# Eight-batch macaron block on one core: two layer tiles moved into the next batch's attention, tile-major normed activations, column-wise output-weight loads, weight splits moved into the schedule

## The reference, cut to what matters

```python
x = x + 0.5 * ffn(layernorm(x), w_router, w_block)
x = x + attn(layernorm(x), Wq, Wk_down, Wv_down, q_to_latent, v_up, Wout)
x = x + 0.5 * ffn(layernorm(x), w_router, w_block)

def ffn(x, w_router, w_block):          # k = 768 of 1024 tokens
    top_idx = top_k(x @ w_router, k)
    out = x; out[top_idx] = gelu(x[top_idx] @ w_block)

def attn(h, ...):                       # 16 heads of 32, latent of 64
    Q = h @ Wq.T; latent_k = h @ Wk_down.T; latent_v = h @ Wv_down.T
    logits = (Q @ q_to_latent) @ latent_k.T / 8, causal
    heads = softmax(logits) @ latent_v @ v_up
    return heads @ Wout.T
```

## Time and profile before

| | |
|---|---|
| runs (median) | 2641.53 us (2641.37 to 2642.27) |
| profiled execution, its own time | 2636.39 us |
| its span in the trace | 2634.7 us |
| mean granted TensorE clock | 0.958 of full speed |
| PE busy | 2351.9 us, 89% |
| DVE busy | 1724.5 us, 65% |
| ACT busy | 1164.1 us, 44% |
| POOL busy | 398.5 us, 15% |

### The profile page before, as it was taken

How to read it: one execution, slowest core, us unless ns; L and a number is a source line. 1 busy time by engine, 2 the same in 40 slices (tenths; PEclk the granted TensorE clock), 3 DMA queues, 4 the chain that set the end, 5 groups by cost and what they waited for, 6 DMA issues and landing times.

```text
span 2634.7 us, 53568 instructions
## 1 busy us (share of the span) xinstructions
PE 2351.9 (89%) x21888; PEld 1462.2 (55%) x21888; DVE 1724.5 (65%) x4806; ACT 1164.1 (44%) x2057; POOL 398.5 (15%) x510
## 2 busy tenths in 40 slices
PE   3769999899998998899988999989999899998976
PEld 2534466545674456745566456654466545674445
DVE  3668656785568855678556866668646785568725
ACT  3325543355434644246433454335543355434442
POOL 0101011112111121021111111111021112111121
PEclk9879999899998999989998999989999899998998
DMA  4100011100111002010020101110011100101000
GB/s 152 64 1 2 2 65 65 65 2 2 65 65 65 2 18 80 33 66 2 21 77 36 63 2 49 49 69 30 2 65 65 65 2 2 65 33 65 2 1 32
DMA packets 42482, 106.19 MB, mean 40 GB/s; under 512 B 2432, under 2 KB 3968, under 8 KB 38400
## 3 DMA queue, kind: packets, MB, share of 16 engines
q1 hardware_dynamic: 42240, 102.77, 11.0%
HBM read 64.49 MB, written 37.75 MB: 39 GB/s over the span
## 4 chain that ended last, share of the span: by engine, by line
PE 74%; DVE 12%; ACT 6%; issue 6%; POOL 1%; DMA 1%; SPq 0%; DVEq 0%; POOLq 0%; ACTq 0%
PE psum L704 30%; PE psum L717 18%; PE psum L823 8%; PE psum L830 7%; PE psum L720 4%; ACT pr L685 4%; DVE psum L958 3%; PE psum L731 3%; PE psum L746 3%; DVE junk L908 2%; DVE junk L906 1%; DVE nt_l L894 1%; DVE part L956 1%; DVE junk L910 1%; ACT nt_h L607 1%
## 5 line engine op out<-in xcount | busy, mean ns | idle before, releaser
L685 ACT ACTIVATE pr<-psum 128x512 f32<-128x512 f32 x1152 | 617.7, 596 | 627.7 <-PE psum L720 627.6
L717 PE MATMUL psum<-qk,qk 32*128 32x512 f32 (+3 forms) x4608 | 526.3, 376 | 100.8 <-ACT pr L685 38.4
L958 DVE CUSTOM_DVE_ANT_0 psum<-psum,mask_b 128x512 f32<-128x512 f32 (+3 forms) x1024 | 473.1, 523 | 142.7 <-PE psum L731 141.2
L717 PEld LDWEIGHTS psum<-qk,qk 32*128 32x128 f32 x4608 | 328.5, 190 | 414.2 <-ACT pr L685 122.8
L731 PE MATMUL psum<-qk,qk 32*128 32x512 f32 (+3 forms) x4608 | 527.6, 380 | 32.2 <-DVE qk L940 12.0
L956 DVE TENSOR_REDUCE part<-psum 128x1 f32<-128x512 f32 x512 | 325.3, 682 | 65.2 <-PE psum L731 63.6
L731 PEld LDWEIGHTS psum<-qk,qk 32*128 32x128 f32 x4608 | 319.9, 192 | 59.2 <-issue 18.2
L823 PE MATMUL psum<-pr,v_sb 128*32 128x512 f32 (+3 forms) x3072 | 316.8, 508 | 1.6 <-ACT acc_sb L607 1.6
L599 POOL TENSOR_SCALAR_AFFINE_SELECT pr<-pr 128x512 f32<-128x512 f32 x256 | 158.1, 636 | 1051.4 <-ACT pr L685 1051.4
L830 PE MATMUL psum<-pr,ones 128*32 128x512 f32 (+3 forms) x3072 | 306.2, 493 | 0.0
L720 PE MATMUL psum<-mrow,minus 1*128 1x512 f32 (+3 forms) x1536 | 223.2, 354 | 0.8 <-issue 0.8
(11 more groups left out here) (115 smaller groups left out, 3382.6 us busy)
## 6 DMA issues: line engine op xcount, KB each, us to landing
x<-x_dram SPq DMA_DIRECT2D x16, 1024.0 KB, 7.0
spill_x<-x SPq DMA_DIRECT2D x16, 1024.0 KB, 5.2
x<-spill_x SPq DMA_DIRECT2D x16, 1024.0 KB, 7.1
out_dram<-x SPq DMA_DIRECT2D x16, 1024.0 KB, 4.7
w_h<-scratch_o SPq DMA_DIRECT2D x7, 1024.0 KB, 4.8
w_l<-scratch_o SPq DMA_DIRECT2D x7, 1024.0 KB, 6.8
w_h<-scratch_q SPq DMA_DIRECT2D x6, 1024.0 KB, 4.9
w_l<-scratch_q SPq DMA_DIRECT2D x6, 1024.0 KB, 8.2
```

The costliest lines, as they stand in the source:

```text
L685: nc.scalar.activation(pr_of(b, g, u)[:, 2 * p + place, :], bank(e, place), ACT.Exp, scale=SCALE).then_inc(exp_ready, 1)
L717: eng.matmul(o, (k_h, k_h, k_l)[t][own, P * j:P * (j + 1)], (q_h, q_l, q_h)[t][own, queries], start=(t == 0 and at == 0), stop=False, skip ...
L958: m = nc.vector.tensor_tensor_reduce(scores, scores, mask_b[:, BANK - w:BANK], 1.0, FAR, ALU.add, ALU.max, top_of)
```

## The change

- **Layer tiles 6 and 7 of the second layer** (`F`, `G` with f = 1) of all batches but the last go from the end of `back(b)` to the first two chunks of group 0 of batch b+1: tile 6 behind the first `S` pair, tile 7 and both gelus behind the second. They use banks 6 and 7. The exp slots are dealt in the order 0, 2, 1, 3, so that the first two units overwrite tiles 0 to 3 only; the exp of unit 0 waits for `F` 3 and that of unit 2 for `F` 7.
- **The tiles of normed activations** become [P, NT, NK, P]: a token tile is one run of 512 elements. What reads 512 tokens at once (`SC`, `LAT`, `Q`) reads four runs of 128.
- **Order in `back`**: the router's `SC`, the maxima units 7 and 8, `SCOL` and the ranks `RT` move. `SCOL` has one `F` fewer ahead of it; `RT` 2 to 7 stand behind `F` 5.
- **Order in `project`**: `CB`, `ST` of tile 7 and the second half's norm factors go behind `T` 3; the `K`, `V`, `Q`, `MX` steps are dealt anew; the output weights are loaded in four column groups of 128, each as soon as `Q` of that group is done.
- **Weight splits** become steps `WS` of the list: router weights ahead of the first `NO`, layer weights behind `T` 4, latent, key/value and output weights ahead of the ranks, query weights behind the norm factors of the second norm.

```diff
     def front(b):
-        out += [("NO", 0, b, 0), ("NO", 0, b, 1)]
+        out += [("WS", 0), ("NO", 0, b, 0), ("NO", 0, b, 1)]
         for i in range(NT):
             out += [("T", 0, b, i)] + ([("NO", 0, b, i + 2)] if i + 2 < NT else [])
             out += [("SC", 0, b, i // TC)] if i % TC == TC - 1 else []
+            out += [("WS", 1)] if i == TC else []
...
     def project(b, left):
-        out += [] if b else [("RT", 0, b, i) for i in range(NT)] + [("RF", 0, b)] + [("GX", 0, b, i) for i in range(NT)]
+        out += [] if b else [("WS", 2), ("WS", 3), ("WS", 4)] + [("RT", 0, b, i) for i in range(NT)] + [("RF", 0, b)]
+        out += [] if b else [("GX", 0, b, i) for i in range(NT)]
         out += layer(0, b, 2) + layer(0, b, 3) + summed(b, 0) + summed(b, 1)
-        out += layer(0, b, 4) + summed(b, 2) + summed(b, 3) + scales(1, b, 0)
+        out += layer(0, b, 4) + summed(b, 2) + summed(b, 3) + scales(1, b, 0) + ([] if b else [("WS", 5)])
...
-        after = [summed(b, 6), summed(b, 7) + scales(1, b, 1), [], []]
+        after = [summed(b, 6), [], [], summed(b, 7) + scales(1, b, 1)]
...
-        for n in range(NQ):
-            out += (keys[0] + splits[0] + keys[1] + splits[1] if n == 0 else keys[n + 1] + splits[n + 1] if n < 3 else [])
-            out += [("Q", b, n, 1)] + (maxima(b, 0, n) if n < 3 else [])
-        out += [("W2", b - 1, "o")] if b else []
-        out += maxima(b, 0, 3)
-        for n in range(TC, NT):
-            out += keys[n] + splits[n] + (maxima(b, 0, 4) if n == TC + 1 else [])
+        loads = [[("W2", b - 1, "o", g)] if b else [] for g in range(NQ)]
+        out += keys[0] + splits[0] + keys[1] + splits[1] + [("Q", b, 0, 1)] + loads[0]
+        out += keys[2] + splits[2] + [("Q", b, 1, 1)] + loads[1] + maxima(b, 0, 0) + splits[3]
+        out += [("Q", b, 2, 1)] + loads[2] + maxima(b, 0, 1) + keys[3] + [("Q", b, 3, 1)] + loads[3] + maxima(b, 0, 2)
+        out += keys[4] + splits[4] + keys[5] + splits[5] + maxima(b, 0, 3)
+        out += keys[6] + splits[6] + keys[7] + splits[7] + maxima(b, 0, 4)
...
     def back(b):
-        out += layer(1, b, 0) + turn(3)[:1] + scales(2, b, 1) + [("SC", 1, b, 0)] + more(maxima, 7)
-        out += [("NO", 2, b, 4), ("NO", 2, b, 5)] + layer(1, b, 1) + turn(4) + turn(5) + more(maxima, 8)
-        out += layer(1, b, 2) + turn(6) + turn(7) + layer(1, b, 3) + [("SC", 1, b, 1)] + more(gathered, 0)
-        out += layer(1, b, 4) + [("SCOL", 1, b)] + more(turned, 0) + [("RT", 1, b, 0), ("RT", 1, b, 1)]
-        for i in range(5, NT):
-            out += layer(1, b, i) + [("RT", 1, b, 2 * (i - TC)), ("RT", 1, b, 2 * (i - TC) + 1)]
+        out += layer(1, b, 0) + turn(3)[:1] + scales(2, b, 1) + [("NO", 2, b, 4), ("NO", 2, b, 5)]
+        out += layer(1, b, 1) + turn(4) + turn(5) + [("SC", 1, b, 0)] + more(maxima, 7) + turn(6) + turn(7)
+        out += layer(1, b, 2) + [("SC", 1, b, 1)] + more(maxima, 8) + layer(1, b, 3) + [("SCOL", 1, b)] + more(gathered, 0)
+        out += layer(1, b, 4) + [("RT", 1, b, 0), ("RT", 1, b, 1)] + more(turned, 0)
+        out += layer(1, b, 5) + [("RT", 1, b, i) for i in range(2, NT)]
+        if b + 1 == B:
+            out += layer(1, b, 6) + layer(1, b, 7)
...
         if b > 0:
+            groups[0][0] += [("F", 1, b - 1, 6)]
+            groups[0][1] += [("F", 1, b - 1, 7), ("G", 1, b - 1, 6), ("G", 1, b - 1, 7)]
...
+        elif k == "F" and e[3] >= 6 and e[2] + 1 < B:
+            own = banks[e] = [e[3]]
...
-        nt_h = [over(f"nt{n}_h", region[n], [P, NK, T], F32R) for n in range(3)]
+        nt_h = [over(f"nt{n}_h", region[n], [P, NT, NK, P], F32R) for n in range(3)]
...
-            return prs[(b + 2) % 3][:, step_nth[b, g, u] % SLOTS, :, :]
+            return prs[(b + 2) % 3][:, (0, 2, 1, 3)[step_nth[b, g, u] % SLOTS], :, :]
...
                 elif k == "W2":
                     if which == "o":
-                        sp.wait_ge(q_done, last_q * (b + 2))
+                        sp.wait_ge(q_done, nth["Q", b + 1, g, 1])
+                        cols = slice(P * g, P * (g + 1))
-                    eng.dma_start(w2_h[:].bitcast(F32), src[0]).then_inc(w2_in, 16)
-                    eng.dma_start(w2_l[:].bitcast(F32), src[1]).then_inc(w2_in, 16)
+                    eng.dma_start(w2_h[:, :, cols].bitcast(F32), src[0][:, :, cols]).then_inc(w2_in, 16)
+                    eng.dma_start(w2_l[:, :, cols].bitcast(F32), src[1][:, :, cols]).then_inc(w2_in, 16)
...
-                    if (g, u) == (0, 0) and b:
-                        act.wait_ge(f_done, nth["F", 1, b - 1, NT - 1])
+                    if g == 0 and u in (0, 2) and b:
+                        act.wait_ge(f_done, nth["F", 1, b - 1, TC - 1 if u == 0 else NT - 1])
...
-                           lambda t, n: t[:, n, c * BANK:(c + 1) * BANK]).then_inc(sc_done, 1)
+                           lambda t, n: t[:, TC * c:TC * (c + 1), n, :]).then_inc(sc_done, 1)
```

More of the change, by code:

```diff
@@ L367, in macaron @@
         parts = [[over(f"qk{n}_{m}", region[n] + 4096 * m, [P, T], F32R) for m in range(8)] for n in range(3)]
-        nt_h = [over(f"nt{n}_h", region[n], [P, NK, T], F32R) for n in range(3)]
-        nt_l = [over(f"nt{n}_l", region[n] + 16384, [P, NK, T], F32R) for n in range(3)]
-        nt_act = [over(f"nt{n}_act", region[n], [P, NK, T]) for n in range(3)]
+        nt_h = [over(f"nt{n}_h", region[n], [P, NT, NK, P], F32R) for n in range(3)]
+        nt_l = [over(f"nt{n}_l", region[n] + 16384, [P, NT, NK, P], F32R) for n in range(3)]
+        nt_act = [over(f"nt{n}_act", region[n], [P, NT, NK, P]) for n in range(3)]
         prs = [over(f"pr{n}", region[n], [P, SLOTS, HQ, BANK]) for n in range(3)]
@@ L475, in macaron @@
         w2_loads = [e for e in sched if e[0] == "W2"]
-        w2_nth = {e: n + 1 for n, e in enumerate(w2_loads)}
-        last_q, last_o = NQ * NC, NT
+        w2_nth = {e: 32 * (n + 1) for n, e in enumerate(w2_loads)}
+        last_o = NT
         block = ctx.enter_context(nc.Block())
@@ L590, in _ @@
                     high, low = nt_of(2, b)
-                    cols = slice(c * BANK, (c + 1) * BANK)
+                    own = slice(TC * c, TC * (c + 1))
                     pool.wait_ge(hsh_ready, nth[e])
-                    nc.gpsimd.tensor_tensor(low[:, g, cols], ht[:, g, cols], high[:, g, cols].bitcast(F32), ALU.subtract
+                    nc.gpsimd.tensor_tensor(low[:, own, g, :], heads_of(g, c), high[:, own, g, :].bitcast(F32), ALU.subtract
                                             ).then_inc(hsl_ready, 1)
@@ L609, in _ @@
             highs = [(wr_h, raw_r), (wb_h, raw_b), (wlat_h, raw_lat), (wkv_h, raw_kv), (w2_h, raw_o), (w2_h, raw_q)]
-            for n, (dst, raw) in enumerate(highs):
-                act.wait_ge(raw_in[n], 16 * (NK if n == 0 else 2 if n == 3 else 1))
-                if n == 5:
-                    act.wait_ge(scr_out, 32)
-                copy(dst[:], raw[:]).then_inc(split, 1)
-                act.wait_ge(split, 2 * n + 2)
             act.wait_ge(consts, 7)
@@ L620, in _ @@
                 k = e[0]
-                if k == "NO":
+                if k == "WS":
+                    n = e[1]
+                    dst, raw = highs[n]
+                    act.wait_ge(raw_in[n], 16 * (NK if n == 0 else 2 if n == 3 else 1))
+                    act.wait_ge(split, 2 * n)
+                    if n == 5:
+                        act.wait_ge(scr_out, 32)
+                    copy(dst[:], raw[:]).then_inc(split, 1)
+                elif k == "NO":
                     s, b, i = e[1:]
@@ L632, in _ @@
                         act.wait_ge(o_done, nth["O", b, i])
-                    copy(nt_of(s, b)[0][:, :, P * i:P * (i + 1)], bank(e).rearrange("p (k t) -> p k t", k=NK)
+                    copy(nt_of(s, b)[0][:, i, :, :], bank(e).rearrange("p (k t) -> p k t", k=NK)
                          ).then_inc(th_ready, 1)
@@ L764, in _ @@
                     pe.wait_ge(tl_ready, nth["T", 2 * f, b, i])
-                    passes(bank(e), nt_of(2 * f, b), (wb_h, wb_l), NK, lambda t, n: t[:, n, P * i:P * (i + 1)],
+                    passes(bank(e), nt_of(2 * f, b), (wb_h, wb_l), NK, lambda t, n: t[:, i, n, :],
                            lambda w, n: w[:, n, :]).then_inc(f_done, 1)
@@ L855, in _ @@
                     (w2_l, raw_o, w2_h), (w2_l, raw_q, w2_h)]
-            def split_low(n):
-                dst, raw, high = lows[n]
-                dve.wait_ge(split, 2 * n + 1)
-                nc.vector.tensor_tensor(dst[:], raw[:], high[:].bitcast(F32), ALU.subtract).then_inc(split, 1)
-            for n in range(len(lows)):
-                split_low(n)
             dve.wait_ge(consts, 7)
@@ L867, in _ @@
                 k = e[0]
-                if k == "ST":
+                if k == "WS":
+                    n = e[1]
+                    dst, raw, high = lows[n]
+                    dve.wait_ge(split, 2 * n + 1)
```

(7 more changed lines are left out.)

21 lines of the change are left out of this document (12 added, 9 removed).

## The result

The kernel after the change takes 2593.23 us (median of four runs, 2591.08 to 2593.58), the kernel before 2641.9 us (four runs, 2641.37 to 2646.28). The ratio is 0.9816, 95% interval 0.9804 to 0.9827: 1.8% faster. That is 9.2 us above the forecast of 2584 and inside its range. The profiled execution took 2591.08 us, with a span of 2589.4, which is 45.3 less than the span before; the sum in the prediction was -57. The medians differ by 48.7 us, as the profiled execution stood 5.1 us under the median before and 2.1 under it after.

The account below looks back on a forecast made before the run. PE, busy 89% of the span, was taken as the bound, leaving its idle and low-clock time to win. Terms -17 - 19 - 4 - 13 - 3, with fractions -57, gave 2579 profiled, 2584 us as median; range 2567 to 2610.

Parts of the forecast that it names:

- The start: Start of the kernel: DVE's first statistics move from 34.80 to 6.3, part given back by the weight splits; -17 us.
- `LAT`: Ahead of `LAT`, seven times: net -1.85 each, and -1.6 more in four that keep the clock; -19 us.
- `Q` to `O`: Second-half `Q` to `O`, seven times: the 1.50 pause is covered, gains together 5, +1 for the clock; -4 us.
- In two of them the pause grows to 2.9 us, near the 3.1 that cost the clock at `LAT`: +1.: At `O` 0: in two of seven batches the longer wait for its bank risks the low clock, +1 us.
- PE waits for it twice more: Between `Q` and `O`: PE waits for DVE ahead of units 3 (1.4 us) and 4 (1.2 us).
- The change of batch: `back` and the batch change, seven times: ranks end 2.55 us earlier, sixth pair starts 1.9 earlier each; -13 us.
- `PV` takes 1.0, the sixth starts at 1445.8: At the batch change, behind the fifth pair: `PV` takes 1.0 us; the sixth pair starts at 1445.8, not 1447.74.
- The change of batch gives back: Rival, chance 0.18: low clock lasts through `F` 7 and two pairs behind; 2.6 us per batch, term +5, time 2602.
- the rival of the table switches, 2593: Rival, chance 0.05: a table switch costs ACT its load time again on the path; 9 us more, 2593.
- Column loads, tile-major reads, table switches: Eight small output-weight loads cost nothing; four-run reads on PE zero; table switches no more than their 1.28 us load.
- both rivals on that read: PE's four-run reads: 27 ns slower each, 2620 us (chance 0.07); slower than before, 2665 at 60 ns (chance 0.05).

Follow-up runs that it names:

- Experiment 9: The kernel before with only the weight splits made steps of the list, at the change's places: 2624.03 us.
- Experiment 4: The kernel before with one line changed, `CB` 7, `ST` 7 and the second half's norm factors behind `T` 3: 2617.99 us.
- Experiment 1: The changed kernel with the ring over eight banks set to the same place at each batch's first `LAT`: 2574.04 us.
- Experiment 3: The changed kernel with the old order of `K`, `V`, `Q` and the maxima, column loads kept: 2584.03 us.
- Experiment 2: The changed kernel with `F` and `G` of tiles 6 and 7 back at the end of `back`: 2567.23 us.
- Experiment 5: The changed kernel with both the ring reset of Experiment 1 and the move back of Experiment 2: 2557.75 us.
- Experiment 6: The changed kernel with `F` 7 directly behind `F` 6, between the first and second pair, gelus behind the second: 2590.95 us.
- Experiment 10: The kernel of Experiment 5 with the second layer's first router `SC` ahead of the third norm's `T` 4: 2557.75 us.

## Why the prediction was right, and where it was wrong

- **The start:** right. -18.6 where -17 was forecast; the first rank and the first `LAT` came 1 and 1.6 us earlier than worked out. The first term had a slip: 34.80 less 6.3 is 28.5, where I wrote 28.3, and PE's first `T` came 28.7 earlier. Experiment 9 shows that the splits' place does it.
- **`LAT`:** right, in both of its parts. The idle time fell to 6.1 us and the clock stayed full: -17.5 where -19 was forecast. Experiment 4 shows it alone.
- **`Q` to `O`:** the gain was right in kind and in its pattern over the batches: 23.94, 25.49, 26.78, 24.84, 23.94, 25.49 and 26.79 us, where before less the forecast gains gives 23.7, 25.1, 26.5, 24.6, 23.7, 25.3 and 26.5. They come to -3.1 and not -5, since each is 0.2 to 0.4 longer than that. The step that failed is the clause "In two of them the pause grows to 2.9 us, near the 3.1 that cost the clock at `LAT`: +1." I had judged the clock by the length of the last pause alone. It fell in four batches and cost 7.2, once behind a pause of only 0.83, while one of 1.49 left it full. Ahead of all seven stand two more pauses, of 1.40 and 1.05 with a unit of maxima behind each. They were in my own working ("PE waits for it twice more"), but not in the price. Experiments 1 and 3 bear this out: without the bank wait, or with the old order and one pause fewer, the clock stays full in seven and in six batches.
- **The change of batch:** the mechanism was right as far as the fifth pair, `F` 7's 4.4 us included. The step that failed is "`PV` takes 1.0, the sixth starts at 1445.8": I had the clock recover with `F` 7 and stay. It recovered, and was lost again behind the two pauses that follow. 14.4 us from the second to the sixth pair on average, where 13.05 was worked out, make 9.4 of the 9.5 us by which this term came out short (-3.5, not -13). The rival *The change of batch gives back* has the right sign and about the right size (+18 was its term against the forecast, 9.5 came), but the wrong place: it kept the clock low through `F` 7, and what was lost was lost behind it. The clock does not explain why the stage grew over before: there 86.3 of its 86.7 us were at the low clock, and 54.4 of 100.8 are now. It grew by the work that was moved into it.
- **What the forecast did not ask:** whether `F` 6 and 7 cost anything where they stood. They lay under the ranks and were free. The 17.6 us gained from `T` to the second pair come from `F` 1's place, the `SCOL` and the ranks, as far as the timelines show; no run has them alone, but experiment 2 keeps them whole (214.7 and 107.7) without the move of `F` 7. Experiments 2 and 5 price the move itself at a loss of 26 and 16 us.
- **The attention:** forecast 0, measured -7.0. The steps there are the same; what moved is the clock. Stage by stage, twice the lost share of the granted clock times the length gives the time at the low clock: 16.8 us before, 2.3 after, and half of the difference is 7.2. Of the 16.8, 10.2 lie around the start of group 3 in three batches, the rest behind the sixth pair, where the low clock of the change of batch ran on. Experiment 6 against the change, and 10 against 5, move this sum by as much the other way, and neither changes a step in it. Why the clock falls there in one kernel and not in the other stays open.
- **The time:** the forecast was missed by 9.2 us and not by some 16 (2600, still in the range) because of this -7.0, which no term foresaw. That is luck. So is it that the rival of the table switches, 2593, names the measured time: its mechanism did not show, as the next point says.
- **Column loads, tile-major reads, table switches:** all three cost nothing beyond their duration, as taken. Two thirds of `Q`'s matmuls take 393 and 391 ns on average where they took 393 and 392, though they now read the activations in four runs, and the first of each three 414 where it took 415. They start 0.23 us apart as before, so both rivals on that read fell. Whether the layout gains anything was not run alone. The Trainium skill, "ScalarE: Activation LUTs", section "What ACT_TABLE_LOAD costs", has a drain added to each switch; here the next activation stands 0.01 us behind each load in the timeline above, and the rival built on it fell with that.

The groups by form after the change have these rows for `Q` (`nt_h`, `nt_l` are the streamed operand; then busy us, mean ns):

```profile
L722 PE MATMUL psum<-nt_h,w_l 128*128 128x512 f32 x256 | 100.5, 393 | 0.0
L722 PE MATMUL psum<-nt_l,w_h 128*128 128x512 f32 x256 | 100.2, 391 | 0.0
```

## What to carry to other kernels

Before moving work out of a stretch, find what sets the end of that stretch. Here DVE's ranks did, PE's two `F`s lay under them for nothing, and moved behind them they cost their full time and two table loads on the path. When a ring of buffers is shared by kinds of steps whose counts per round change, work out anew which step meets which buffer in every round: one line that resets the ring was worth 17 us by the spans and 19 by the medians. And when a change leaves pauses one behind the other, price the low clock for all of them, not for the last alone.
